# Separate operation lists for even and odd steps on four engines of a fused RWKV and local-attention kernel

## The reference

```python
x = x + _L0_attn_ref(_layernorm(x), ...)     # RWKV: projections r, k, v, a scan over time, group norm, W_o
def _L0_ffn_ref(x, ...):                     # applied to _layernorm(x), and added to x
    for l in range(2):
        h = shift_token(x); q, k, v = split(h @ wqkv[l])
        q, k = rotary_xpos(l2norm(q) * qs, l2norm(k) * ks)
        x = x + local_attention(q, k, v) @ wo[l]      # 8 heads of 64, windows of 128 with the one before
        h = layernorm(shift_token(x)) * lg + lb
        a, g = split(h @ w1[l] + b1[l]); x = x + (a * gelu(g)) @ w2[l] + b2[l]
```

## Time and profile before

| | us |
|---|---|
| median of 3 runs | 2856.45 (2856.03 to 2857.04) |
| profiled execution, own time | 2855.33 |
| its span | 2853.2 |
| PE busy in the span | 2750.0 (96%) |
| DVE, ACT, POOL busy | 2325.1, 2284.3, 1637.9 |

### The profile page before, as it was taken

The page is one execution under the profiler, slowest core; times in us unless marked ns, Lnnn a source line. Parts: engine busy times, 40 slices in busy tenths (PEclk is TensorE's granted clock), DMA queues, the critical chain, the costliest instruction groups (busy, mean ns, idle before and its releaser), DMA issues.

```text
span 2853.2 us, 75604 instructions
## 1 busy us (share of the span) xinstructions
PE 2750.0 (96%) x27108; PEld 2496.1 (87%) x27108; DVE 2325.1 (81%) x6459; ACT 2284.3 (80%) x5557; POOL 1637.9 (57%) x1652
## 2 busy tenths in 40 slices
PE   7999948999999999999999999999999999999998
PEld 6888836899999999999999899899999999999998
DVE  3979978988888888888888787888888888888884
ACT  4979956788888888888888788888888888888885
POOL 2323317666666666666666565666666666666653
PEclk9999979999999999999999999999999999999999
DMA  3252111121121112111111213111111111111111
GB/s 101 65 186 72 40 59 58 51 57 57 48 55 53 48 55 57 57 50 53 53 50 50 85 57 102 50 50 50 46 50 47 49 46 48 50 50 50 50 39 46
DMA packets 211334, 166.75 MB, mean 58 GB/s; under 512 B 21522, under 2 KB 206612, under 8 KB 209940
## 3 DMA queue, kind: packets, MB, share of 16 engines
q1 hardware_dynamic: 139284, 127.82, 14.8%
q10 hardware_dynamic: 71680, 34.10, 4.2%
HBM read 110.89 MB, written 42.58 MB: 54 GB/s over the span
## 4 chain that ended last, share of the span: by engine, by line
PE 84%; DVE 8%; issue 3%; ACT 2%; DMA 2%; SPq 1%; POOL 1%; ACTq 0%; DVEq 0%; POOLq 0%
PE ps L397 31%; PE ps L396 17%; PE ps L363 10%; PE ps L472 7%; PE ps L460 6%; PE ps L488 4%; DVE Sm L1112 3%; PE ps L445 3%; PE ps L498 2%; DVE Ar L1083 1%; DVE oTl L1135 1%; PE ps L524 1%; PE ps L423 1%; DMA oF<-ro_scratch 1%; PE ps L350 1%
## 5 line engine op out<-in xcount | busy, mean ns | idle before, releaser
L761 ACT ACTIVATE Sm<-Sm,nb 128x256 f32<-128x256 f32 (+1 forms) x1024 | 503.1, 496 | 1.4 <-DVE nb L1112 0.7
L1112 DVE CUSTOM_DVE_ANT_0 Sm<-ps,mask,sc 128x256 f32<-128x256 f32 (+1 forms) x1024 | 420.3, 475 | 77.3 <-PE ps L460 37.7
L1257 POOL TENSOR_TENSOR rs<-rs,mhalf 128x8 f32<-128x8 f32 x256 | 422.1, 1649 | 14.2
L1345 POOL TENSOR_TENSOR uTl<-Gl,uTh 128x512 fp32r<-128x512 f32 (+1 forms) x192 | 212.1, 1105 | 327.8 <-ACT uTh L834 219.7
L396 PE MATMUL ps<-zTh,W1h 128*128 128x256 f32 (+1 forms) x1408 | 375.6, 288 | 0.1
L741 ACT ACTIVATE sq<-ps 128x512 f32<-128x512 f32 x256 | 151.5, 592 | 269.4 <-PE ps L397 265.7
L396 PE MATMUL ps<-zTh,W1l 128*128 128x256 f32 (+1 forms) x1408 | 365.7, 282 | 0.0
L1184 DVE SCALAR_TENSOR_TENSOR Gl<-ps,vecs,Gl 128x256 f32<-128x256 f32 (+1 forms) x384 | 172.0, 476 | 219.8 <-PE ps L396 118.8
L397 PE MATMUL ps<-WQh,hTh 128*128 128x512 f32 x768 | 339.3, 442 | 2.8 <-ACT hTh L735 2.8
L397 PE MATMUL ps<-WQl,hTh 128*128 128x512 f32 x768 | 302.9, 394 | 0.0
L1356 POOL TENSOR_TENSOR Ar<-Ar,Br 128x512 f32<-128x512 f32 x128 | 164.6, 1286 | 219.9 <-DVE Br L1085 219.9
(11 more groups left out here) (190 smaller groups left out, 8645.7 us busy)
## 6 DMA issues: line engine op xcount, KB each, us to landing
oF<-ro_scratch ACTq DMA_DIRECT2D x256, 128.0 KB, 3.1
tb<-tab SPq DMA_DIRECT2D x128, 128.0 KB, 2.3
xc<-x SPq DMA_DIRECT2D x32, 256.0 KB, 3.0
rwkv_scratch<-rw SPq DMA_DIRECT2D x32, 256.0 KB, 2.7
rk<-rwkv_scratch SPq DMA_DIRECT2D x64, 128.0 KB, 2.3
xin<-x SPq DMA_DIRECT2D x64, 128.0 KB, 2.3
x_scratch<-x SPq DMA_DIRECT2D x64, 128.0 KB, 1.7
y_scratch<-os SPq DMA_DIRECT2D x64, 128.0 KB, 4.2
```

The source lines that it names most:

```text
L761: act.activation(Sm[:, h, c0:c1_], Sm[:, h, c0:c1_], ACT.Exp, bias=nb[:, h:h + 1], scale=-1.0, accum_out=sm[:, n % 2, h:h + 1]).then_inc(S ...
L1112: dve.tensor_tensor_reduce(Sm[:, h, c0:c1_], PS[:, bank["scores", n, q, h % 2], (h // 2 % 2) * 256 + c0:(h // 2 % 2) * 256 + c1_], mask[:, ...
L1257: return pool.tensor_tensor(ap, ap, mhalf[:, 0:ap.shape[-1]], ALU.pow)
L1345: pool.tensor_tensor(uT[1][:, j, :], Gl[:, g, :], uT[0][:, j, :].bitcast(F32), ALU.subtract).then_inc(S["ul"], 1)
```

## The change

Every engine's step body is split into an even and an odd list. In PE's odd step the last four stages (q's transposes `qkT 0`, v's projection `qkv 2`, `hT`, `pre`) are gone and stand in the following even step: the first two ahead of `pv`, `hT` between `pv` and `wo`, `pre` after the first of the `turn`s. The `turn`s of the even step are spread among the MLP's parts. On DVE, in odd steps, the second of two `z_norm`s stands between `rope 0` and `sums`; `x2_out` of the next unit and `z_stats` close the list; `pre_x1` stands a step later; `oT_lo` stands between the two `qk_lo`s. On ACT the third `gelu` stands ahead of the second `u_hi`, and `pre_norm` of odd steps follows `qk_hi 0`. POOL has nearly all work of a pair in one list that runs one step late.

```diff
@@ psum_order2 and tensor_program, even steps (the same order in both)
+                if t % 2 == 0:
+                    turn_qk(t - 4, 0)
+                    qkv(t - 3, 2)
+                    pv(t - 6, 0)
+                    pv(t - 6, 1)
+                    turn_h(t - 2)
+                    wo_mm(t - 7)
+                    turn_p(t - 5, 0)
+                    pre_mm(t - 1)
+                    mlp((t - 11) // 2, 0)
+                    turn_p(t - 5, 1)
+                    mlp((t - 11) // 2, 1)
+                    turn_p(t - 5, 2)
+                    mlp((t - 11) // 2, 2)
+                    turn_p(t - 5, 3)
+                    scores(t - 4, 0)
...
@@ tensor_program, odd steps
-                    turn_qk(t - 3, 0)
-                    qkv(t - 2, 2)
-                    turn_h(t - 1)
-                    pre_mm(t)
@@ vector_program, odd steps
+                    z_norm(t - 9)
+                    pre_x1(t - 1)
+                    o_norm(t - 6)
+                    o_sums(t - 5)
+                    x2_out(t - 7)
+                    x3_out(t - 13)
+                    x3_out(t - 12)
...
+                    qk_lo(t - 3, 1)
+                    oT_lo(t - 6)
+                    qk_lo(t - 3, 0)
+                    zero_h2(t - 7)
+                    rope(t - 2, 0)
+                    z_norm(t - 8)
+                    sums(t - 2)
+                    hT_lo(t - 1)
+                    z_stats(t - 7)
+                    x2_out(t - 6)
@@ scalar_program, even steps
+                    gelu((t - 11) // 2, 1)
+                    u_hi((t - 11) // 2, 0)
+                    p_out(t - 5, 2)
+                    oT_hi(t - 6)
+                    gelu((t - 11) // 2, 2)
+                    u_hi((t - 11) // 2, 1)
+                    p_out(t - 5, 3)
...
@@ gpsimd_program, odd steps
...
+                    zT_lo(t - 10)
+                    nT_lo(t)
+                    os_out(t - 12)
+                    rot(t - 2)
```

More of the change, by code:

```diff
@@ L135, in psum_order2 @@
[L135 to L148, removed]
+    if t % 2 == 0:
+        if live(4):
+            yield "qkT", t - 4, 0
+        if live(3):
+            yield "qkv", t - 3, 2
+        if live(6):
+            yield "pv", t - 6, 0
+            yield "pv", t - 6, 1
+        if live(2):
+            yield "hT", t - 2
+        if live(7):
+            yield "wo", t - 7
+        if live(5):
+            yield "turn", t - 5, 0
+        if live(1) and t - 1 < NG:
+            yield "pre", t - 1
+        if live(11):
+            yield "gate", (t - 11) // 2, 0
+            yield "up", (t - 11) // 2, 0
+        if live(5):
+            yield "turn", t - 5, 1
+        if live(11):
+            yield "gate", (t - 11) // 2, 1
+            yield "up", (t - 11) // 2, 1
+        if live(5):
+            yield "turn", t - 5, 2
+        if live(11):
+            yield "gate", (t - 11) // 2, 2
+            yield "up", (t - 11) // 2, 2
+        if live(5):
+            yield "turn", t - 5, 3
+        if live(4):
+            yield "scores", t - 4, 0, 0
+            yield "scores", t - 4, 0, 1
+            yield "scores", t - 4, 1, 0
+            yield "scores", t - 4, 1, 1
+        if live(2):
+            yield "qkv", t - 2, 1
+        if live(5):
+            yield "rT", t - 5
+        if live(3):
+            yield "qkT", t - 3, 1
+        if live(2):
+            yield "qkv", t - 2, 0
+        if live(3):
+            yield "qkT", t - 3, 0
+        if live(2):
+            yield "qkv", t - 2, 2
+        if live(1):
+            yield "hT", t - 1
+        if live(10):
+            yield "zT", t - 10
+        if live(0) and t < NG:
+            yield "pre", t
+    else:
+        if live(6):
+            yield "pv", t - 6, 0
+            yield "pv", t - 6, 1
+        if live(7):
+            yield "wo", t - 7
+        if live(10):
+            yield "zT", t - 10
+        if live(13):
+            yield "w2", t - 13
+        if live(5):
+            yield "turn", t - 5, 0
+        if live(12):
+            yield "w2", t - 12
+        if live(5):
+            yield "turn", t - 5, 1
+            yield "turn", t - 5, 2
+            yield "turn", t - 5, 3
+        if live(4):
+            yield "scores", t - 4, 0, 0
+            yield "scores", t - 4, 0, 1
+            yield "scores", t - 4, 1, 0
+            yield "scores", t - 4, 1, 1
+        if live(2):
+            yield "qkv", t - 2, 1
+        if live(5):
+            yield "rT", t - 5
+        if live(3):
+            yield "qkT", t - 3, 1
+        if live(2):
+            yield "qkv", t - 2, 0
@@ L839, in live @@
                     return 0 <= t - d < U
[L841 to L869, removed]
@@ L1201, in live @@
                     return 0 <= t - d < U
[L1203 to L1216, removed]
```

385 lines of the change are left out of this document (235 added, 150 removed).

## The result

The changed kernel takes 2927.76 us (median of 4 runs, 2923.67 to 2928.19) against 2856.24 for the kernel before on the same chip (4 runs): a ratio of 1.0246, interval 1.0234 to 1.0258, or +71.5 us. The forecast was 2880, with a range of 2840 to 2898. The sign and the collision came out; the size was three times the forecast. The profiled execution took 2923.67 us, its span is 2921.6, 68.4 above the span before.

What follows compares the result with a forecast made beforehand. PE was taken to bound the kernel, with 0.56 us a pair waiting in layer one. Layer one +12.5, layer two +13.5 and change of layer -2 gave +24 on 2856.45: 2880 us, range 2840 to 2898.

Steps and rivals of the forecast that it cites:

- The bound: Both layers: PE is the bound; layer one waits about 0.56 us a pair, layer two has nothing to win.
- The 1.9 us: DVE, odd steps, layer one: z_norm's two halves wait for POOL's k and q adds, 1.9 us instead of 0.5.
- the first rival: Kernel gets faster: z_norm's halves go through together, costing 0.9 instead of 1.9; 2843 us, chance 0.27.
- Gate part 1: PE, layer one: waits 0.7 us for the bank that o_norm's first operation frees, giving +0.2 a pair.
- The odd scores, layer one: PE's odd scores wait for x2_out, starting at 1427.2 instead of 1426.28: +0.9 a pair; middle taken, 0.5.
- Layer two: Late cast delays x2_out and the odd scores: +0.5 us a pair, between 0.1 and 1.2; 27 pairs, 13.5 us.
- both further collisions: Layer two's high end, 1.2 a pair: two more collisions of 0.4, the other z_norm and oT_lo in the even step.
- The change of layer: Between the layers, PE's 4.24 us wait for x2_out shrinks: -2 us, between -4 and 0.
- the first and last steps: First ten steps wait for ACT's exponentials, last ten for the MLP's chain, in both orders: 0, within 3.
- `pre`'s term: PE, layer one: the waits at pre (0.46 us) and at wo's entry (0.1) go, -0.56 a pair.
- no wait of `pre` for the rope: Sign expected in the changed profile: PE's pre no longer waits for DVE's rope.
- the high ends' 54: Upper limit of the range: high ends 22 + 32 = +54 us, of which 45 was allowed, giving 2902.

Runs made afterwards that it cites:

- e11: Kernel before with one line of the change, u_tail moved behind the sums: 2841.31 us, ratio 0.9947.
- e5: Changed kernel with z_norm behind hT_lo, oT_lo ahead of k's rope and x2_out ahead of o_norm and o_sums, in odd steps: 2837.22 us, ratio 0.9936.
- e2_znorm_oT: Changed kernel with, in odd steps, z_norm moved behind hT_lo and oT_lo back ahead of k's rope: 2854.56 us, ratio 0.9991.
- e7: Changed kernel with only oT_lo moved back ahead of k's rope in odd steps: 2902.99 us, ratio 1.0163.
- e4: Kernel before with, in every other step, the next step's leading z_norm moved between q's rope and the sums: 2873.92 us, ratio 1.0062.
- e1: Changed kernel with only z_norm moved behind hT_lo, ahead of z_stats, in odd steps: 2857.77 us, ratio 1.0004.
- e3: Changed kernel with one more wait on POOL: q's add of odd units starts only when z_norm is done: 2880.77 us, ratio 1.0086.
- e6: Changed kernel with only x2_out moved ahead of o_norm and o_sums in odd steps: 2905.37 us, ratio 1.0173.
- e10: Kernel before with x2_out and the zeroing of h2 moved ahead of o_norm in every step: 2857.09 us, ratio 1.0001.

## Why the prediction was right or wrong, point by point

**The bound.** Right: PE was the bound, 0.56 a pair in layer one was waiting, and layer two had nothing to win. e11 takes 0.58 of it and e5 0.63, and then nothing is left.

**The 1.9 us.** Right to the hundredth in layer one (1.90). For layer two I had 1.56 and 0.7; measured were 1.49 and 0.73. That the halves pass together, the first rival, didn't occur.

**Gate part 1.** Forecast 0.7 of waiting for `o_norm`'s bank; the rows show 0.62, and against e2_znorm_oT the first half of the pair is 0.64 longer. Right.

**The odd scores, layer one: the first term that failed.** The prediction had a low end (+0.2, gate part 1 alone) and a high end (+0.9, the chain down to `x2_out`) and took the middle, 0.5, for a collision of `pre_y` that might go. Measured: +0.95. The chain had been worked out, 1.34 late of the 1.9; measured from the end of q's rope to the end of `x2_out` it is 30.22 instead of 28.78, 1.44 late. The relief that I allowed for came in full, `pre_y` takes 0.42 instead of 0.81, but I had set nothing against it. Two collisions that I hadn't placed ate it, of `oT_lo` in the even step (0.95 instead of 0.69) and of `o_norm`'s second operation (1.11 instead of 0.69, in the row at 1411.95), and so did the reciprocal ahead of `x2_out`. So the middle of the range was mis-sized and its high end, 0.9, was right. 0.45 times 26 pairs are 11.7 us.

**Layer two: the second term that failed.** Forecast +0.5 between 0.1 and 1.2, measured +1.19. The cast came late as forecast, and both further collisions that I had put at the high end occurred (the other `z_norm` 0.84 instead of 0.34, `oT_lo` in the even step 0.94 instead of 0.69). But I followed the delay to one consumer, the odd scores behind `x2_out`, and not to `pv` of the odd step, whose bank k's rope frees. That rope stands earlier in DVE's list, so it has less to spare. e7 isolates it: with `oT_lo` away, the wait at `pv` goes and 0.72 a pair with it. The other 0.44 is at the odd scores, but behind ACT, not behind `x2_out`; that is read from the rows, and no run tests it. 0.69 times 30 pairs are 20.7 us.

**How slack is spent.** The middle of a range is the wrong guess for delays on one chain, and the runs suggest why. In layer two the 1.50 of e4 cost 0.42, the 1.49 of e7 cost 0.51 (against e2_znorm_oT), `oT_lo`'s 0.73 alone (e1) cost 0.05, and both together, 2.22, cost 1.23. All fit one slack of about 1 us (0.98 to 1.08): it is free, and the rest is paid in full. This is a fit, not something that a run isolates: e4 pays at `pv`, e7 at the odd scores, the changed kernel at both. e3, with 0.51 + 0.73 = 1.24, paid 0.41, so its slack is 0.8; the fit is no better than 0.3. My 2.3 late minus the 1.0 that I had myself read as spare at `x2_out` gives 1.3, near the 1.2 that I called the high end.

Where the slack lies can be seen in e2_znorm_oT: the masked max of the even step starts 1.11 after the scores, so it follows the scores and not gelu, and gelu's last product ended 0.4 earlier. In the changed kernel it starts 1.6 after them in layer one and 2.7 in layer two: it now follows gelu, and the pair, as I read it, is no longer set by PE but by a loop over the other engines: in layer one `hT_hi`, gelu, max, ropes, sums, `x2_out`, max, ropes, `z_norm`, sums and `hT_hi` again. In layer two `x2_out` can't be in it, since e6 gained nothing there. That e4 lost so little in layer one is the same in other numbers: its loop took 38.50 us against the 38.43 that PE took anyway, and the changed kernel's 39.37, since `x2_out` ended 26.9 after the `hT_hi` that starts gelu and not 25.9 as in e4 (in e6, 25.0).

**Pairs and ends.** I counted 25 and 27 undisturbed pairs and there were 26 and 30, which is 2 us at the forecast's prices. The change of layer gave 1.1 of the 2 forecast. For the first and last steps I put 0 within 3; they lost 5.0 and 3.7. e5_x2_first has 186.1 us there together against 184.7 before and 193.4 in the changed kernel, so most of it goes with the same three moves; `x2_out`'s alone gave 2.8 in e6 and 5.9 from e2 to e5. These stretches differ by up to 3 us between kernels whose difference shouldn't touch them (e10 has 91.2 at the start, the kernel before 88.5), so which move does it stays open.

**`pre`'s term.** Right in size, but not in the sum: -0.56 a pair came only in e11 and e5. In the changed kernel 0.33 of it stayed (0.25 at `pre`, 0.08 at `wo`). The forecast sign "no wait of `pre` for the rope" so failed, though the list of waits no longer shows it: the rope stands earlier in DVE's list, but the late max holds it back. In e2_znorm_oT, with the collisions gone, the pair of layer one is 0.18 shorter and no more, as the wait had moved to the odd scores (1.85 us behind the twelve transposes instead of 1.40). To ask what is late next once that stall goes would have found `x2_out` behind `o_norm` there.

**The sum.** With what was measured: 26 times 0.95 and 30 times 1.19 are 60.4, a few pairs off the usual add 1.5, the ends 7.6 (-1.1, 5.0 and 3.7), the change of layer takes 1.1: 68.4. Of the 44 us that were missing, the two layer prices are 32 (11.7 and 20.7), the ends 8, the number of pairs, the odd ones and the change of layer the rest. The range failed with them: I cut the high ends' 54 to 45 because "both layers' worst collisions hardly come together". The same instruction in the same place made both, so they came together by necessity. Even uncut, the high ends would have stopped at 2910.

## What to carry to other kernels

Where a loop has a busy engine beside a chain through the others, a delay on the chain was free up to a slack and, as the fit above has it, then paid in full; add all delays of one round first and take the slack off once, instead of halving each. Follow a late operation to every consumer in its list, the earliest ones first (here the bank that a rope frees, ahead of the one that `x2_out` frees), and through the other engines' lists (here ACT's `zf`). A VectorE operation of the kinds that were held here (`z_norm`'s halves, or one that reads two SBUF tiles like `oT_lo`; not the reduction of the sums, which kept its 1.21) shouldn't stand between the operation that releases a large GpSimd one and the operation that a chain waits for; two such instructions in the wrong gap cost 70 us of this kernel, 2.4%, and moving them behind the sums and `hT_lo` gave it back.

## What the runs showed of the hardware

Small operations are caught too. In e2_znorm_oT the scalar maximum over 128x16 behind the sums takes 0.67 (0.67 to 0.69 in 24 places) where it takes 0.17 in the changed kernel, and ends 0.03 after POOL's q add. The reduction ahead of it reads 128x1024 beside the first 0.61 of the same add and takes 1.22; in e3_qadd_waits's rows it overlaps 0.99 of an add and takes 1.21. DVE first, then POOL:

```profile
1396.28 1.22 DVE L1194 TENSOR_REDUCE ss<-sq 128x16 f32<-128x1024 f32 x1
1397.53 0.67 DVE L1199 TENSOR_SCALAR rs<-ss 128x16 f32<-128x16 f32 x1
...
1399.18 0.34 DVE L1273 TENSOR_SCALAR z<-x,mv,r 128x128 f32<-128x128 f32 x1
...
1396.89 1.28 POOL L1494 TENSOR_TENSOR Ar<-Ar,Br 128x512 f32<-128x512 f32 x1
1398.29 1.65 POOL L1393 TENSOR_TENSOR rs<-rs,mhalf 128x8 f32<-128x8 f32 x1
```

The last row of each engine shows a second thing: half a `z_norm` passes in 0.34 beside POOL's pow, which runs for 1.65 over 8 columns. So what counts isn't that POOL is busy, but with which operation. POOL's two adds never paid: they took 1.26 to 1.33 in the seven traces up to e5_x2_first. Another operation of POOL did, where DVE's came first: in the kernel before, `nT_lo` started at 1414.30, 0.16 behind DVE's `oT_lo`, and took 1.13, as the usual one of that step did in layer one, where in the other step of the pair it took 0.75.
